# DLRM tower with a compressed interaction network: the tower's first layer computed in parts, and a GpSimd tile handed to VectorE in every fourth unit

## What is computed

```python
xk = x0                                   # x0 = e: (1024, 32, 16)
for W in (W0, W1, W2):                    # W: (32, fields of xk, 64)
    xk = relu(einsum('bmd,bhd,mhk->bkd', x0, xk, W))
    outs.append(sum(xk, axis=2))          # (1024, 64)
h = concatenate([outs[0], outs[1], outs[2], dense_ctx], axis=1)    # (1024, 208)
h = maximum(h @ W_top1 + b_top1, 0)       # 512 wide
h = maximum(h @ W_top2 + b_top2, 0)       # 256 wide
y = h @ W_top3                            # (1024, 1)
```

## Time and profile before

| | us |
|---|---|
| median of 3 runs | 630.08 (626.87 to 632.82) |
| the profiled execution | 628.08 |
| its span, first to last instruction | 626.2 |
| PE busy | 573.1 (92%) |
| DVE busy | 547.3 (87%) |
| ACT busy | 467.3 (75%) |
| POOL busy | 457.8 (73%) |
| mean granted clock of TensorE | 0.986 of full speed |

### The profile page before, as it was taken

How to read it: one execution, slowest core, us unless ns; L and a number is a source line. 1 busy time by engine, 2 the same in 40 slices (tenths; PEclk the granted TensorE clock), 3 DMA queues, 4 the chain that set the end, 5 groups by cost and what they waited for, 6 DMA issues and landing times.

```text
span 626.2 us, 9918 instructions
## 1 busy us (share of the span) xinstructions
PE 573.1 (92%) x2620; PEld 193.7 (31%) x2620; DVE 547.3 (87%) x298; ACT 467.3 (75%) x3337; POOL 457.8 (73%) x353
## 2 busy tenths in 40 slices
PE   0389879999999998999999999999998999999998
PEld 0144322323232333333232323323343333233332
DVE  0389997999999999999999999999998999999500
ACT  0146677979797969689797969696978959796521
POOL 6777887889896988888888979798788866174000
PEclk9999889999999998999999999999898999999999
DMA  4878795939495776949394949587593939363100
GB/s 98 248 224 303 288 408 183 416 123 412 149 392 205 300 280 235 363 161 415 118 416 127 411 173 360 222 310 288 198 397 102 416 124 421 134 270 66 28 0 0
DMA packets 39187, 153.17 MB, mean 245 GB/s; under 512 B 8493, under 2 KB 18585, under 8 KB 23771
## 3 DMA queue, kind: packets, MB, share of 16 engines
q1 hardware_dynamic: 23956, 144.33, 58.7%
q0 software_dynamic: 8192, 2.11, 3.3%
q10 hardware_dynamic: 6983, 6.11, 3.0%
HBM read 147.60 MB, written 4.92 MB: 244 GB/s over the span
## 4 chain that ended last, share of the span: by engine, by line
POOL 31%; PE 25%; issue 16%; DVE 13%; ACT 3%; DMA 2%; POOLq 0%; SPq 0%; DVEq 0%
PE acc L638 20%; POOL rows L398 18%; POOL prod_pool L411 12%; DVE prod L448 12%; PE x L729 2%; ACT x L504 2%; PE x L698 1%; DMA spread<-x_scratch 1%; ACT relu_out L516 1%; DMA rows<-table,ids_sb 1%; PE x L720 1%; PE x L706 1%; PE acc L698 0%; ACT x_pool L504 0%; PE acc L706 0%
## 5 line engine op out<-in xcount | busy, mean ns | idle before, releaser
L448 DVE TENSOR_TENSOR prod<-spread,x 128x2048 f32<-128x2048 f32 (+2 forms) x277 | 536.7, 2006 | 17.3 <-DMA spread<-x_scratch_half 7.1
L638 PE MATMUL acc<-prod,w 128*64 128x512 f32 (+1 forms) x2076 | 460.2, 580 | 49.5 <-DVE prod L448 38.6
L398 POOL DMA_INDIRECT rows<-table,ids_sb x256 | 242.7, 948 | 81.2 <-issue 76.8
L638 PEld LDWEIGHTS acc<-prod,w 128*64 128x64 f32 x2076 | 151.2, 140 | 341.7 <-issue 251.9
L411 POOL TENSOR_TENSOR prod_pool<-spread,x_pool 128x1024 f32<-128x1024 f32 (+1 forms) x93 | 214.9, 2346 | 40.6 <-ACT x_pool L504 40.1
L516 ACT ACTIVATE relu_out<-acc 128x16 f32<-128x16 f32 x960 | 161.1, 359 | 8.2 <-DVE xt L437 5.4
L516 ACT ACTIVATION_READ_ACCUMULATOR relu_out<-acc 128x1 f32 x960 | 161.6, 385 | 0.0
L504 ACT ACTIVATE x<-acc 64x512 f32<-64x512 f32 (+1 forms) x136 | 74.1, 545 | 89.4 <-PE acc L638 87.7
L523 ACT ACTIVATE relu_out<-relu_out 128x16 f32<-128x16 f32 x544 | 110.4, 388 | 0.0
L523 ACT ACTIVATION_READ_ACCUMULATOR relu_out<-relu_out 128x1 f32 x544 | 110.1, 374 | 0.0
L638 PE MATMUL acc<-prod_pool,w 128*64 128x512 f32 (+1 forms) x372 | 94.7, 586 | 0.3 <-POOL prod_pool L411 0.3
(11 more groups left out here) (25 smaller groups left out, 33.6 us busy)
## 6 DMA issues: line engine op xcount, KB each, us to landing
spread<-x_scratch SPq DMA_DIRECT2D x120, 1024.0 KB, 8.8
first<-x_scratch SPq DMA_DIRECT2D x15, 512.0 KB, 7.7
spread<-x_scratch_half SPq DMA_DIRECT2D x14, 512.0 KB, 7.1
rows<-table,ids_sb POOLq DMA_INDIRECT x256
x_scratch<-xt ACTq DMA_DIRECT2D x15, 256.0 KB
w<-w ACTq DMA_DIRECT2D x2, 512.0 KB, 4.8
spread<-x_scratch_half SPq DMA_DIRECT2D x4, 256.0 KB, 4.6
spread<-wt SPq DMA_DIRECT2D x2, 384.0 KB, 4.5
```

The costliest lines, as they stand in the source:

```text
L398: nc.gpsimd.indirect_dma_start(rows[u % 2][:, j * D:(j + 1) * D], None, table, bass.IndirectOffsetOnAxis(ap=index, axis=0)).then_inc(gathe ...
L448: nc.vector.tensor_tensor(prod[:, at:at + count, 0:n], tiles(u, t, count), x[:, 0:n].rearrange("p (a n) -> p a n", a=1).to_broadcast([P, c ...
L638: last = nc.tensor.matmul(parts(to[K * blk:K * blk + K, 0:n]), w, side(moving[:, 0:2 * n], blk), start=start, stop=stop)
```

## The change

GpSimd has tiles 5 and 6 only, not 7, in layer 3 of units 2, 6, 10 and 14; VectorE makes tile 7 there, in a step of its own. The ring has 10 slots instead of 12, prod_pool 3 instead of 4; relu_out of layer 3 shares its buffer with that of layer 1, and w_1b lies in prod_pool. The room goes to the tower's first weights, which ScalarE's queue now loads at the start, and to h_1.

The tower's first layer is cut into batches of 128 columns. Of the first three batches, a part (one block t of one batch) is computed behind layer 1 of unit u + 1, for u from 5 to 15, on TensorE into x0 (`early_h1`), and ScalarE adds the bias and the relu behind `after_1(u + 1)`. Unit 14 has two parts, the others one. Behind the last product stand: the second layer of half 0 over the 384 columns of those batches, the first layer's last batch, the second layer of half 1 over 384 columns, the second layer of the last batch, and the third layer, whose sums go to the acc banks. Of the second layer's matmuls nothing is moved ahead of the last product. Semaphores of ScalarE on its own work (`buffer_free`) guard the shared buffer.

```diff
...
-RING = 12
+RING = 10
...
-POOL_SLOTS = 4
-EARLY = 4
-AHEAD = 7
+POOL_SLOTS = 3
...
-    return () if (layer, u) in ((2, 0), (3, 0), (2, 1)) else (5, 6, 7)
+    if (layer, u) in ((2, 0), (3, 0), (2, 1)):
+        return ()
+    return (5, 6) if layer == 3 and u % 4 == 2 else (5, 6, 7)
...
-    return (0, 2), (2, 2), (4, 1), (8, 2), (10, 2), (12, 2), (14, 2)
+    rest = ((8, 2), (10, 2), (12, 2), (14, 2))
+    return ((0, 2), (2, 2), (4, 1)) + (rest if 7 in pool_tiles(layer, u) else ((7, 1),) + rest)
...
+BATCH = COLS // 4
+EARLY_PARTS = {5: (0, (0,)), 6: (0, (1,)), 7: (0, (2,)), 8: (0, (3,)), 9: (1, (0,)), 10: (1, (1,)), 11: (1, (2,)),
+               12: (1, (3,)), 13: (2, (0,)), 14: (2, (1, 2)), 15: (2, (3,))}
+SOON = 3 * BATCH
...
-        square = sb("square", [M, N])
+        square = sb("square", [P, N])
...
-        relu_out = [sb(f"relu_out{i}", [P, BLK]) for i in range(3)]
+        relu_out = [sb(f"relu_out{i}", [P, BLK]) for i in range(2)]
+        relu_out.append(relu_out[0])
...
+        w_top1 = sb("w_top1", [P, 3, H1])
+        h_1 = sb("h_1", [P, H1 // P, 2, SOON])
...
         def to_h1(t, g):
-            return (x1, x0, x2)[t][:, g * BLK:(g + 1) * BLK] if t < 3 else acc[g][:, :]
+            return x0[:, g * BLK:g * BLK + BATCH]
+        def to_h1_last(t, g):
+            return x2[:, g * BLK + t * BATCH:g * BLK + (t + 1) * BATCH]
         def to_h2(t, g):
             return (x1, x0)[g][:, t * BLK:(t + 1) * BLK]
         def to_y(g):
-            return x2[M * g:M * g + 1, g * BLK:(g + 1) * BLK]
+            return acc[g][M * g:M * g + 1, :]
...
-            for g in range(2):
-                own = slice(64 * g, 64 * g + K)
-                sp.dma_start(w_top1[own, :, :], wt1[0:3 * K, :].rearrange("(l k) n -> k l n", k=K)).then_inc(tower_in, 16)
-                own = slice(64 * g, 64 * g + D)
-                sp.dma_start(w_dense[own, :], wt1[3 * K:3 * K + D, :]).then_inc(tower_in, 16)
-                sp.dma_start(dense[own, :], dense_t[g]).then_inc(tower_in, 16)
-            sp.dma_start(w_top2[:, :, :], wt2.rearrange("(s p) n -> p s n", p=P)).then_inc(tower_in, 16)
+            sp.dma_start(w_top2[:, :, :], wt2.rearrange("(s p) n -> p s n", p=P)).then_inc(w_top2_in, 16)
...
+            def early_h1(u):
+                batch, parts_of = EARLY_PARTS.get(u, (0, ()))
+                for t in parts_of:
+                    n = sum(len(EARLY_PARTS[v][1]) for v in EARLY_PARTS if v < u) + parts_of.index(t) + 1
+                    act.wait_ge(h1_soon_mm, n)
+                    for g in range(2):
+                        last = nc.scalar.activation(h_1[:, t, g, batch * BATCH:(batch + 1) * BATCH], to_h1(t, g), ACT.Relu,
+                                                    bias=b_1[:, t:t + 1])
+                    last.then_inc(h1_soon_out, 1)
...
+            def early_h1_kept(u):
+                n = sum(len(EARLY_PARTS[v][1]) for v in EARLY_PARTS if v < u)
+                if n:
+                    act.wait_ge(h1_soon_out, n)
             def base_tile(u):
                 act.wait_ge(first_in, 16 * (u + 1))
+                early_h1_kept(u - 1)
...
+            for g in range(2):
+                act.dma_start(w_top1[64 * g:64 * g + K, :, :], wt1[0:3 * K, :].rearrange("(l k) n -> k l n", k=K)).then_inc(tower_in, 16)
+                act.dma_start(w_dense[g], wt1[3 * K:3 * K + D, :]).then_inc(tower_in, 16)
+                act.dma_start(dense[g], dense_t[g]).then_inc(tower_in, 16)
...
                 after_1(u + 1)
+                early_h1(u)
                 sum_2(u)
...
-            act.wait_ge(small_in, 48)
-            for t in range(H1 // P):
-                for g in range(2):
-                    act.wait_ge(h1_mm, 2 * t + g + 1)
-                    nc.scalar.activation(h_1[:, t, g, :], to_h1(t, g), ACT.Relu, bias=b_1[:, t:t + 1]).then_inc(h1_out, 1)
+            for g in range(2):
+                act.wait_ge(h1_mm, 2 * (H1 // P - 1) + g + 1)
+                for t in range(H1 // P):
+                    nc.scalar.activation(h_1_last[:, t, g, :], to_h1_last(t, g), ACT.Relu, bias=b_1[:, t:t + 1]).then_inc(h1_out, 1)
...
+            def sums_in(to, t, l, columns):
+                for g in range(2):
+                    own = slice(64 * g, 64 * g + K)
+                    last = nc.tensor.matmul(to(t, g), w_top1[own, l, t * P:(t + 1) * P], z[own, l, columns],
+                                            start=l == 0, stop=l == 2)
+                return last
+            def dense_in(to, t, columns):
+                for g in range(2):
+                    nc.tensor.matmul(to(t, g), w_dense[g][:, t * P:(t + 1) * P], dense[g][:, columns], start=False, stop=False)
+            def early_h1(u):
+                batch, parts_of = EARLY_PARTS.get(u, (0, ()))
+                columns = slice(batch * BATCH, (batch + 1) * BATCH)
+                for t in parts_of:
+                    n = sum(len(EARLY_PARTS[v][1]) for v in EARLY_PARTS if v < u) + parts_of.index(t)
+                    if n:
+                        pe.wait_ge(h1_soon_out, n)
+                    else:
+                        pe.wait_ge(tower_in, 96)
+                    for l in range(2):
+                        pe.wait_ge(summed[l], batch_units(batch))
+                        sums_in(to_h1, t, l, columns)
+                    dense_in(to_h1, t, columns)
+                    pe.wait_ge(summed[2], batch_units(batch))
+                    sums_in(to_h1, t, 2, columns).then_inc(h1_soon_mm, 1)
...
                 layer_1(u + 1)
+                early_h1(u)
...
-            pe.wait_ge(tower_in, 112)
+            def to_layer_2(g, t, columns, h, done):
+                for s in range(H1 // P):
+                    if done:
+                        pe.wait_ge(h1_out, g * (H1 // P) + s + 1)
+                    last = nc.tensor.matmul(to_h2(t, g)[:, columns], w_top2[:, s, t * P:(t + 1) * P], h[:, s, g, :],
+                                            start=s == 0, stop=s == H1 // P - 1)
+                if done:
+                    last.then_inc(h2_mm, 1)
+            soon, late = slice(0, SOON), slice(SOON, COLS)
+            pe.wait_ge(h1_soon_out, 3 * (H1 // P))
+            pe.wait_ge(w_top2_in, 16)
+            for t in range(H2 // P):
+                to_layer_2(0, t, soon, h_1, False)
             for t in range(H1 // P):
                 for l in range(2):
                     pe.wait_ge(summed[l], UNITS)
-                    sums_in(t, l)
-                dense_in(t)
+                    sums_in(to_h1_last, t, l, late)
+                dense_in(to_h1_last, t, late)
                 pe.wait_ge(summed[2], UNITS)
-                sums_in(t, 2)
-            def to_layer_3(g):
-                for s in range(H2 // P):
+                for g in range(2):
+                    own = slice(64 * g, 64 * g + K)
+                    nc.tensor.matmul(to_h1_last(t, g), w_top1[own, 2, t * P:(t + 1) * P], z[own, 2, late],
+                                     start=False, stop=True).then_inc(h1_mm, 1)
+            for t in range(H2 // P):
+                to_layer_2(1, t, soon, h_1, False)
+            for g in range(2):
+                for t in range(H2 // P):
+                    to_layer_2(g, t, late, h_1_last, True)
+            pe.wait_ge(small_in, 48)
+            for s in range(H2 // P):
+                for g in range(2):
                     pe.wait_ge(h2_out, 2 * g + s + 1)
                     last = nc.tensor.matmul(to_y(g), w_top3[:, s:s + 1], h_2[:, s, g, :],
                                             start=s == 0, stop=s == H2 // P - 1)
-                last.then_inc(y_mm, 1)
-            pe.wait_ge(small_in, 48)
-            for g in range(2):
-                pe.wait_ge(h1_out, 2 * (H1 // P - 1) + g + 1)
-                for t in range(H2 // P):
-                    for s in range(H1 // P):
-                        last = nc.tensor.matmul(to_h2(t, g), w_top2[:, s, t * P:(t + 1) * P], h_1[:, s, g, :],
-                                                start=s == 0, stop=s == H1 // P - 1)
-                    last.then_inc(h2_mm, 1)
-                    if (t, g) == (0, 1):
-                        to_layer_3(0)
-            to_layer_3(1)
+                    if s == H2 // P - 1:
+                        last.then_inc(y_mm, 1)
```

More of the change, by code:

```diff
@@ L145, with batch_units @@
 PLACES, POOL_PLACES, BANKS = places(), pool_places(), banks()
+BATCH = COLS // 4
+EARLY_PARTS = {5: (0, (0,)), 6: (0, (1,)), 7: (0, (2,)), 8: (0, (3,)), 9: (1, (0,)), 10: (1, (1,)), 11: (1, (2,)),
+               12: (1, (3,)), 13: (2, (0,)), 14: (2, (1, 2)), 15: (2, (3,))}
+SOON = 3 * BATCH
+def batch_units(batch):
+    return sum(1 for u in range(UNITS) if z_at(u) < (batch + 1) * BATCH)
 def made(layer, u, i=-1):
@@ L206, in build @@
         warm = sb("warm", [1, 1])
+        w_top1 = sb("w_top1", [P, 3, H1])
+        h_1 = sb("h_1", [P, H1 // P, 2, SOON])
+        w_dense = [square[64 + M * g:64 + M * g + D, 0:H1] for g in range(2)]
```

(31 more changed lines are left out.)

21 lines of the change are left out of this document (14 added, 7 removed).

## The result

| | before | changed |
|---|---|---|
| median of 20 runs | 629.43 us (626.87 to 634.29) | 633.12 us (630.68 to 636.80) |
| ratio, with its 95% interval | | 1.0054 (1.0037 to 1.0071) |
| span of the profiled execution | 626.2 us | 630.0 us |
| mean granted clock of TensorE | 0.986 | 0.986 |

The changed kernel is slower by 0.5%, some 3.5 us. The forecast was +6.9 us, 637.0. The range of 629 to 647 holds the time, but the change itself is about half of what I worked out, and it is less than the 1% that I took as the bound of "slower".

The account below looks back on a forecast made before the run. VectorE, TensorE and GpSimd were taken as nearly full, each the bound by turns. Steady part +2.0, stall +13.7 and tail -8.8 gave +6.9 us, 637.0 us; range 629 to 647, own range 632 to 643.

Parts of the forecast that it names:

- The stall in unit 14: Unit 14: TensorE's second part waits for ScalarE's answer behind after_1(15), same place in x0; +13.7 us (12 to 16).
- The clock penalty: Unit 14, behind TensorE's pause: 20 instructions at half clock take 6.0 us instead of 4.3, adding 1.7 us.
- The tail: From TensorE's last product to the end: 27.9 us against 36.7, so -8.8 us.
- if each pair waits for its own load, 0.19; I take 0.15: Price of a pair of 128-column instructions on TensorE: 0.15 us, between full overlap and load length; a part 1.9 us.
- 8 instructions, 3.5 (two times the 1.82 of 621.90): Last layer in the tail: eight TensorE instructions at twice the earlier 1.82 us, 3.5 us.
- small matmuls are cheap: Rival: a 128-column pair costs 0.107 us, a part 1.5, tail -11.6; +1.0 us in all, 631; chance 0.22.
- The steady part: Units before the stall: tile steps, late x2 and fewer waits for gathered rows together cost +2.0 us.
- 1.5 + 3.3 + 4.5 - 7.3: Steady units: gather waits kept 1.5, three VectorE steps 3.3, late x2 4.5, less 7.3 us of earlier VectorE waits.
- VectorE's waits for gathered rows under 2 us: Sign in the changed profile: VectorE's waits for gathered rows sum to under 2 us; 1.5 of 7.3 us kept.
- the lateness of x2: Units 5 to 13: a part makes x2 0.9 us late, paid five times, 4.5 us.
- each time its lag is cleared: GpSimd, units 2, 6, 10, 14: one product less, 2.35 us, clears its lag; VectorE's waits fall from 7.3 to 1.5 us.
- The rival on the other side: Rival: unit 14's stall does not decide; -6.8 us, 623, or 618 with cheap matmuls; chance 0.10.

Follow-up runs that it names:

- the kernel with the earlier answer: Changed kernel with ScalarE's activations for the parts moved ahead of the 32 sums of after_1; 627.86 us, ratio 0.9987 to the kernel before.
- the kernel with two places: Changed kernel with unit 14's two parts side by side in x0, both computed before ScalarE reads; 619.56 us, ratio 0.9833 to the kernel before.
- the part repeated: Kernel with unit 14's parts side by side in x0, each part's matmuls issued twice; 629.08 us, ratio 1.0003 to the kernel before.
- the handover alone: Kernel before with only GpSimd's tile 7 of layer 3 given to VectorE in units 2, 6, 10 and 14; 632.16 us, ratio 1.0043.
- the handover in units 5 and 12: Kernel before with only GpSimd's tile 7 of layer 3 given to VectorE in units 5 and 12; 626.28 us, ratio 0.9957.

## Why the prediction was right in part, and where it failed

**The stall in unit 14: right.** The forecast had TensorE idle for nearly 10 us between two parts, ended by ScalarE's activation of h_1, then a stretch at half clock. It was 9.66 us, with that releaser. The path in numbers: the second part started at 525.37 (forecast 523.8, and in this execution all of it is 2.1 us later, from unit 14's layer 3 at 512.13 instead of 509.99); layer 3 of unit 15 came 14.8 us late in its step (forecast 14.0). The clock penalty was mis-sized at 1.7 us. It measured 3.4. I had taken it from the earlier trace rows, behind a pause of 1.3 us, and the pause here was seven times as long; behind the 4.36 us of the kernel with the earlier answer it was 2.5. That the stall was paid is shown by the kernel with two places, 13.9 us faster.

**The tail: the failed term.** I gave it -8.8 us and it was -12.4; this alone is the difference between +6.9 and +3.3. Two steps of its sum failed. One is "if each pair waits for its own load, 0.19; I take 0.15": a pair measured 0.107 and an instruction on all rows 0.114, which is 2.0 us of the 3.6. The other is the last layer as "8 instructions, 3.5 (two times the 1.82 of 621.90)", which put them in a row where they run two at a time: 1.86, another 1.6 us. The tail also fell below the 25 us that the forecast had named as a sign of being wrong.

| in the tail | forecast | measured |
|---|---|---|
| half 0, 384 columns, 16 instructions | 5.1 | 5.36 |
| four blocks of 128 columns | 6.4 | 5.36 |
| half 1 on 384 columns, then 32 instructions on 128 | 9.9 | 8.93 |
| last layer | 3.5 | 1.86 |
| copies, waits, changes, to the end | 3.0 | 2.76 |
| sum | 27.9 | 24.27 |

A pair of instructions of 128 columns costs 0.107 us: in the part repeated, 1.29 us are eight pairs (0.86) and two changes of shape (0.21 each). The 32 instructions on all 128 rows took 3.66 us, 0.114 each. So the price is a quarter of that at 512 columns, although the load's 0.186 us from start to end is longer than this; no time of the loads shows beside it. The changes between shapes were right at 0.2 (a part of 1.48 us has three: 0.62). The rival "small matmuls are cheap" was right in its mechanism, and the part of 1.5 us was its number; my own of 1.9 was not. Its time of 631 is within the runs, in part by luck: it had the stall too low (12.8, where the two stages measured 14.1 together) and the last layer too high, and these went against each other.

The Trainium skill (TensorE: Matmul & The Clock Gate, section LDWEIGHTS) gives 107 ns for a load of 128 columns; by that rule, which the prediction weighed, the estimate for a part is 1.5 us. The trace agrees with the outcome, though it does not prove the rule: load by that rule and stream by the trace have the same length here.

**The steady part: right in size by two errors.** The forecast of +2.0 was 1.5 + 3.3 + 4.5 - 7.3. The measured one, +1.1, is the difference of two sums over twelve units of 33.57 us: before 7.5 us over them, changed 8.6. In the latter are the single steps at 3.4 (forecast 3.3). The waits for gathered rows stayed at 3.46 and some 0.4 us of small ones with them, where I kept 1.5; "VectorE's waits for gathered rows under 2 us" did not come. And the lateness of x2 was three times some 0.43 us, 1.3 instead of 4.5. Of the 0.9 us each that I had, the part, 0.4 us shorter, explains nearly all; that it came three times and not five was not tried apart. The step "each time its lag is cleared" was the wrong one in the first: by its place in the traces the lag that hurts follows a late gather, and a tile given away in unit 2 or 10 clears nothing, as the handover alone (1.0043) and the handover in units 5 and 12 (0.9957) show. Only for the wait of 1.3 us ahead of unit 12 this account does not hold.

**What was costed at nothing** was nothing: the smaller ring and slots (0.9991, with its interval around 1), and the loads of the weights at the start, as far as the scatter of the start lets one see. In unit 14 itself the ring did stop VectorE, for 8.48 us, as the prediction had it.

**The chances.** The forecast's sign was right and the size too large by a factor of two, and the chance of "slower by over 1%", 0.52, went to a case that did not come. The rival on the other side (the stall not paid, 618 with cheap matmuls) turned out to be the time of the kernel in which the stall is removed: 619.56.

## What to carry to other kernels

When work is cut into small parts and slipped into another engine's slack, two parts in one unit need two places, or the second waits for the answer to the first, and that answer stands as late as the answering engine's program has it: here 9.7 us of pause, 13.9 us of time, more than the whole of what the change gains elsewhere. A wait that comes at fixed points wants its relief in the unit ahead of it; the same tile given away on a regular beat cost 0.4%, and at the right two units it gained 0.4%. Matmuls of 128 columns, standing in a row, cost a quarter of those of 512 here, although a load lasts longer from start to end; each change of shape counts apart. And what took 1.82 us alone took hardly longer, 1.86, with the other half's matmuls beside it, so look for pairs before you add prices up.

## What was not expected of the hardware

- Two gathers of 256, always 112 apart in the queue, start behind 1.8 to 3.9 us of idle time without a releaser in the profile, in every kernel of the study. Four more gathers ahead of them move both by 20 places, not by 0 or 4.
- After a pause of 9.7 us TensorE worked at a granted clock of 0.50 for some 7 us (525.4 to 532.6), and that cost 3.4 us; after one of 4.4 us it cost 2.5, after one of 1.3 us 1.7.
- Pairs of fp32 instructions of 128 columns, one of each half of the rows, follow each other at 0.107 us, though each load shows 0.186 us from start to end. Each change between 64 and 16 rows adds 0.21 us.
- Eight instructions of one weight column and 512 columns of data into two acc banks took 1.86 us, where four into x2 took 1.82, in either order of the halves: they start in pairs, and the pairs are 0.43 us apart.
